# Cross-attention and expert layer: constants awaited singly, input loads reordered, two products moved ahead

## The reference

```python
kv   = ctx @ W_k.T + b_k                      # (b, 512, 128)
out  = layernorm(x) @ kv                      # (b, 512, 128)
sim  = out @ kv.T * 512 ** -0.5               # (b, 512, 512)
sim  = (sim - mean(sim)) * rsqrt(var(sim) + 1e-6) * ln_gamma + ln_beta
x    = x + softmax(sim)
n    = layernorm(x)
s, i = top_k(n @ Wg.T, 2);  w = softmax(s)    # two experts for each row
x    = x + sum_e w[e] * ((silu(n @ W1[e].T) * (n @ W2[e].T)) @ W3[e].T)
```

## Time and profile before

| | |
|---|---|
| Median of three runs | 385.76 us (385.14 to 386.96) |
| Profiled execution | 385.42 us, span 383.4 us |
| PE busy | 360.2 us, 94% of the span |
| DVE, ACT, POOL busy | 251.5, 234.5, 165.3 us |
| Chain that ended last | PE 77%, POOL 6%, issue 6%, DVE 4%, DMA 3%, ACT 2% |
| DMA | 57.61 MB, mean 150 GB/s |
| Mean granted clock of TensorE | 0.956 |

### The profile page before, as it was taken

One profiled execution on the slowest core, in us unless ns is written; L12 is line 12 of the kernel. 1 busy time (PEld: TensorE's weight loads), 2 busy tenths in 40 slices (PEclk: granted clock), 3 DMA queues, 4 the chain that ended last, 5 costly groups with the idle time before them and its releaser, 6 DMA issues.

```text
span 383.4 us, 8249 instructions
## 1 busy us (share of the span) xinstructions
PE 360.2 (94%) x2348; PEld 240.3 (63%) x2348; DVE 251.5 (66%) x647; ACT 234.5 (61%) x412; POOL 165.3 (43%) x193
## 2 busy tenths in 40 slices
PE   6889999998997999999999999999999999999981
PEld 5556767677965566566666666666666666666640
DVE  1267858887567965766676767575757576766660
ACT  1246857666356988857565666666666666575750
POOL 2116664868815034254434343435252534343331
PEclk9999999997558999999999999999999999999996
DMA  6999999898923034435353535354544444453424
GB/s 231 398 418 304 363 414 332 320 303 274 370 102 84 28 57 69 99 55 96 73 100 67 107 62 109 62 106 62 105 68 99 70 97 80 89 82 86 82 29 55
DMA packets 22121, 57.61 MB, mean 150 GB/s; under 512 B 4864, under 2 KB 4992, under 8 KB 20544
## 3 DMA queue, kind: packets, MB, share of 16 engines
q0 software_dynamic: 8736, 20.53, 29.7%
q1 hardware_dynamic: 11184, 20.17, 14.8%
q10 hardware_dynamic: 2160, 16.38, 11.5%
HBM read 38.17 MB, written 18.91 MB: 149 GB/s over the span
## 4 chain that ended last, share of the span: by engine, by line
PE 77%; POOL 6%; issue 6%; DVE 4%; DMA 3%; ACT 2%; POOLq 1%; DVEq 0%; ACTq 0%
PE bank L1308 36%; PE bank L1329 16%; PE bank L1299 4%; PE bank L1148 4%; PE bank L1319 3%; PE bank L1351 3%; PE bank L1169 2%; PE bank L1191 2%; PE bank L1057 2%; PE bank L1203 1%; DMA ng_s<-n_table,gidx 1%; DMA out<-kvj_s,sidx 1%; POOL rstd L429 1%; PE bank L1140 1%; POOL wrow L457 1%
## 5 line engine op out<-in xcount | busy, mean ns | idle before, releaser
L1308 PE MATMUL bank<-Wp,kvg_s 128*128 x480 | 78.2, 313 | 1.7 <-DVE kvg_s L1001 1.5
L995 DVE SCALAR_TENSOR_TENSOR stage<-W,w3sc,stage 128x512 f16<-128x512 f16 x99 | 71.1, 746 | 5.7 <-ACT stage L674 5.7
L1308 PE MATMUL bank<-Wp,kv_s 128*128 x456 | 74.3, 313 | 0.3
L1329 PE MATMUL bank<-stage,n_s 128*128 128x512 f16 (+1 forms) x297 | 69.6, 379 | 1.5 <-issue 1.5
L674 ACT ACTIVATE stage<-W,w3sc 128x512 f16 x99 | 67.3, 716 | 0.7 <-DVE w3sc L985 0.7
L1308 PEld LDWEIGHTS bank<-Wp,kvg_s 128*128 128x128 f16 x480 | 46.7, 98 | 29.0 <-issue 4.4
L526 POOL DMA_INDIRECT out<-oT_s,sidx x20 | 31.7, 1587 | 72.4 <-ACT oT_s L705 61.3
L1308 PEld LDWEIGHTS bank<-Wp,kv_s 128*128 128x128 f16 x456 | 44.4, 98 | 26.1 <-issue 2.7
L526 POOL DMA_INDIRECT out<-kvj_s,sidx x19 | 30.0, 1581 | 65.8 <-ACT kvj_s L705 63.4
L1022 DVE TENSOR_TENSOR n_s<-bank,n_s 128x384 f16<-128x384 f32 x33 | 18.4, 558 | 55.0 <-ACT n_s L687 53.3
L510 POOL DMA_INDIRECT ng_s<-n_table,gidx x39 | 41.2, 1056 | 22.2 <-issue 11.3
(11 more groups left out here) (196 smaller groups left out, 556.7 us busy)
## 6 DMA issues: line engine op xcount, KB each, us to landing
Wp<-in_w ACTq DMA_DIRECT2D x7, 1408.0 KB, 8.9
W<-in_w ACTq DMA_DIRECT2D x8, 768.0 KB, 6.6
W<-in_x SPq DMA_DIRECT2D x12, 256.0 KB, 9.7
out<-W SPq DMA_DIRECT2D x12, 256.0 KB, 8.6
stage<-in_xT SPq DMA_DIRECT2D x2, 1024.0 KB, 7.8
Wp<-in_xT SPq DMA_DIRECT2D x2, 1024.0 KB, 9.3
n_table<-n_s SPq DMA_DIRECT2D x8, 256.0 KB, 6.0
n_table<-x_s SPq DMA_DIRECT2D x8, 256.0 KB, 8.4
```

The lines of the kernel that those rows point to most:

```text
L995: eng.scalar_tensor_tensor(w3p[r][:, W3N + c * D:W3N + (c + 1) * D], W3[:, bass.ds(e * W3N + c * D, D)], w3sc[:, bass.ds(e, 1)], w3p[r][:, ...
L1308: mm = eng.matmul(bank[2 * which + r][:, 0:H], n_, w_, start=(c == 0 and k == 0), stop=(c == DC - 1 and k == 2))
L1329: mm = eng.matmul(ybank(t)[:, :], h_, w_, start=(c == 0 and k == 0), stop=(c == HC - 1 and k == 2))
```

## The change

Five edits:
- POOL makes `ones16` first, and TensorE starts its warm-up after one constant; it waits for all of them behind the warm-up. The counts in POOL's and ACT's waits go up by one.
- SP's key group is loaded in the order bias, context, weights. `w12[0]` is loaded ahead of x row 2 and no longer behind `wg_s`; `xT[1]` goes behind x row 2.
- For batch 0, both `outs` come before `gram` on TensorE, and `o_evac` before `gram_copy` on ACT.
- `squares(0)` comes before `sims(0, 1)` in slot n = 0.
- `weight_gram(0)` comes before `turn_keys(1)` in slot n = 1.

```diff
-            for dst, src in ((wk_s[:, :], wkT), (ctx_s[:, 0:N], ctxT[:, 0:N]), (bk_s[:, :], bk)):
+            for dst, src in ((bk_s[:, :], bk), (ctx_s[:, 0:N], ctxT[:, 0:N]), (wk_s[:, :], wkT)):
                 eng.dma_start(dst, src).then_inc(s_key, 16)
...
             for g in range(XAHEAD - 1):
                 if g == 2:
                     load_ctx(1)
+                    eng.dma_start(wst[0], w12[0]).then_inc(s_w[0], 16)
+                if g == 3:
                     eng.dma_start(xT_s[1], xT[1]).then_inc(s_xT[1], 16)
                 eng.dma_start(x_s[g], xrows[g]).then_inc(s_xl[g], 16)
             eng.dma_start(wg_s[:, :, :], wgT).then_inc(s_cin, 16)
-            eng.dma_start(wst[0], w12[0]).then_inc(s_w[0], 16)
             load_ctx(2)
...
         def _(eng):
+            eng.memset(ones16[:, :], 1.0).then_inc(s_const, 1)
             eng.memset(ident[:, :], 0.0).then_inc(s_const, 1)
...
-            eng.wait_ge(s_const, 6)
+            eng.wait_ge(s_const, 7)
...
-            eng.memset(ones16[:, :], 1.0).then_inc(s_const, 1)
...
-            eng.wait_ge(s_const, 4)
+            eng.wait_ge(s_const, 5)
             eng.activation(spare_a[:, 0:1], half[:, :], ACT.Exp)
...
             kvj_evac(0)
+            o_evac(0)
             gram_copy(0)
-            o_evac(0)
             batches(slot)
...
                 ba, ia = lead(b, i, 2)
+                if n == 0:
+                    squares(0)
                 if real(ba) and i != 2:
                     sims(ba, ia)
-                if i == 3 and real(b + 1):
+                if i == 3 and real(b + 1) and n > 0:
                     squares(b + 1)
                 if i == 3 and real(b + 2):
                     keys(b + 2)
+                if n == 1:
+                    weight_gram(0, 0, W12N // P)
                 if i == 0 and real(b + 1):
                     turn_keys(b + 1)
...
                 for k, slots in enumerate(GRAM_SLOTS):
-                    if n in slots:
+                    if n in slots and k > 0:
...
+            eng.wait_ge(s_const, 1)
+            warm(ones16[:, :], WARM_START)
             eng.wait_ge(s_const, NCONST)
-            warm(ones16[:, :], WARM_START)
             eng.wait_ge(s_key, 16 * 3)
             keys(0)
             warm(ones16[:, :], 2 * WARM_SLOT)
             turn_keys(0)
             warm(ones16[:, :], WARM_SLOT)
-            gram(0)
             outs(0, 0)
             outs(0, 1)
+            gram(0)
             gram_outs(0)
             sims(0, 0)
             eng.wait_ge(s_cin, 16)
```

## The result

Four executions of the changed kernel took 391.9 to 393.43 us, median 392.78, beside 385.66 us of the kernel before (four executions, 385.14 to 386.96). The ratio is 1.0178 (95% interval 1.0146 to 1.021): slower by some 7 us. The prediction was 389.7 us, with a range of 384.2 to 393.0. The profiled execution took 392.89 us with a span of 391.0, against 385.42 and 383.4: 7.5 us more.

The account below looks back on a forecast made before the run. TensorE's chain was taken as the bound. Gate at 23.5, work 8.5 and clock 2.4 put outs of batch 1 at 34.4 against 30.13, 4.3 us later: 385.42 becomes 389.7 us, own range 388 to 391.5, wide range 384.2 to 393.0.

Parts of the forecast that it names:

- The gate: TensorE's wait for wg_s after sims(0,0): reached at 17.05, open at 23.5 us, bounds 20.4 and 23.7.
- The difference made by ACT's load: ACT's w12[1], 1408 KB, going ahead of wg_s would delay its landing by 3.3 us.
- lower end: Earliest landing of wg_s, 20.4 us, if w12[1] starts only after it; taken from w12[0]'s landing before.
- The Trainium skill's rule on packets: An engine drains some 9 to 17 descriptors per queue turn; w12[1] goes through whole, gate at 23.7.
- The clock: TensorE idle 6.4 us at the gate drops to half clock; 4.8 us to recover, cost 2.4, bounds 0 and 8.5.
- The sum: Start of outs of batch 1: 23.5 + 8.5 + 2.4 = 34.4 against 30.13, 4.3 us later.
- Nothing gives it back: After outs of batch 1, the 4.3 us delay should reach the end of the kernel.
- The clock stays down: Rival: half clock persists behind the gate; ten microseconds at half cost 5.0, 392.3 us; whole 8.5, 395.8; chance 0.12.
- The early start gains nothing with the gate closed: Warm-up after one constant starts TensorE 2.6 us earlier, but gains nothing if it then waits for wg_s.
- Squares and weight products first: Behind the gate, weight products cover the 1.64 us wait for kv_s; work to outs of batch 1 is 8.5 us.
- `outs` before `gram`: In batch 0, ACT copies oT_s under gram, saving another 0.3 us; sims(0,0) ends at 17.05.
- The rival of the small load passing: wg_s gets past the large loads, gate at 17.05; w12[1] then holds outs of batch 1: 381.9 us, chance 0.09.

Follow-up runs that it names:

- Numbers 1 and 2: Changed kernel with wg_s loaded ahead of the x rows: 383.76 us; changed kernel with the wait for wg_s moved to the first router product: 383.61 us.
- number 6: Changed kernel with ACT's issue of w12[1] moved from the head to the end of its slot 0: 394.03 us in one execution.
- number 5: Kernel before with only w12[0] loaded ahead of x row 2 and xT[1] behind it: 388.17 us, ratio 1.0048.
- number 3: Changed kernel with 132 warm-up products between the first sims and the wait for wg_s: 389.55 us, ratio 1.0116.
- number 7: Changed kernel with wg_s loaded ahead of the x rows and the 48 warm-up products again behind all constants: 385.07 us, ratio 0.9985.
- number 11: Kernel before with only ones16 made first and the 48 warm-up products behind one constant: 383.67 us, ratio 0.9953.
- number 10: Changed kernel with wg_s ahead of the x rows, and sims(0,1) ahead of squares(0), turn_keys(1) ahead of weight_gram(0) again: 382.85 us.
- number 1: Changed kernel with the 16 KB load of wg_s issued ahead of the x rows: 383.76 us, ratio 0.9948.
- number 9: Changed kernel with wg_s ahead of the x rows, w12[1] issued before ACT's copy of outs, and more warm-up around the first gather: 381.22 us.

## Why the prediction was right or wrong

The measured median lies 3.1 us above the forecast, outside the narrower range of 388 to 391.5 us and 0.2 us inside the edge of the wide one. The mechanism was right. Two terms of the sum were too small, and one loss was not in it.

- *The gate*: right in place, cause and sign. Numbers 1 and 2 show it from two sides. Sized 23.5, measured 24.85, beyond my upper end of 23.7. The difference made by ACT's load was right (3.3 forecast, 3.4 in number 6), and so was its start (first packets at 18.3 forecast, 18.5 measured). Too low was the lower end: 20.4 forecast, 20.70 measured in number 5 (where 0.10 MB of `w12[1]` had gone) and 21.45 in number 6. I took it from `w12[0]`'s landing with the same bytes ahead. That assumes that a load lands when the bytes ahead of it and its own have moved, and these come to 5.98 MB. At the landing the queue had moved more: 6.50 MB for `w12[0]` before, 6.54 for `wg_s` in number 5, 6.79 in number 6 and 6.83 in the changed kernel. So parts of the loads behind had passed already. The 0.25 MB by which numbers 5 and 6 differ are 0.6 us at the 0.4 MB a microsecond that the queue moved there. Why more passed in one than in the other stays open.
- *The Trainium skill's rule on packets* (DMA: Bandwidth & Descriptors, Queues, rings and completion order): by the rule and by my value all of `w12[1]` went ahead, and that came true: q10 moved 1.39 of the load's 1.44 MB in 18.5:22.5, before `wg_s` landed. The counts don't tell whether the two queues took turns packet by packet or in longer turns, neither these (128 against 193) nor those of the earlier trace rows, from which the prediction reads "close to one by one".
- *The clock*: right that it falls, and number 3 shows that it costs. The mis-sized term is how long it stays down behind the gate: 4.8 us taken from the warm-up at the start, 6.8 measured; cost 3.4 and not 2.4, and 3.3 by number 3. The 4.8 us was one sample of a time that varies: the same 48 products took 5.11 us before and 4.41 in the changed kernel, and behind the gate of number 6 the clock was back after 5.3 us. So the kind of work behind the gate is not shown to be what made it longer. The Trainium skill (TensorE: Matmul & The Clock Gate, What's actually happening) calls the lower clock the default state, released by activity, and the prediction says that the rows of 90 us agree. They don't: TensorE was busy for 26.46 of 27 us at 0.51.
- *The sum*: 34.4 forecast for `outs` of batch 1, 36.71 measured; 1.35 from the gate, 1.0 from the clock. The work itself, 8.5, was right: number 3 has it at full clock, 8.50.
- *Nothing gives it back*: right, 6.58 us at 36.71 became 7.5 at the end. That something is added behind, the short fall of the clock at 127 us (0.9 us), was no step of mine.
- *The clock stays down* (0.12): this rival's 392.3 is nearest to the measured time, but not by its own sum: it had 5.0 us for the clock and 23.5 for the gate.
- *The early start gains nothing with the gate closed*: too mild. With it ACT issues `w12[1]` before `wg_s` has passed; in number 5, without it, the gate opened at 20.7 and not at 24.85. With the gate open it is worth 1.3 us (number 7); alone, with the old loads and 0.7 us of wait at the gate, 2 us (number 11).
- *Squares and weight products first*: counted at 1.6 us of TensorE's time; that wait is gone. With the gate open the order was worth 0.36 us at `outs` (number 10), since `w12[1]` was due next. In the changed kernel it lay behind the gate, which is why the sum could keep it.
- *`outs` before `gram`, and the new order of the key group*: neither was tried alone. Both act ahead of the gate, where TensorE came at 17.3 (17.05 forecast).
- *The rival of the small load passing*: its premise was false, but its consequence was checked by number 1: forecast 381.9, measured 383.8.

## What to carry to other kernels

Before moving anything earlier, list the waits that cost nothing today and their slack in us; a full stop for a small load behind large ones (2.9 us of slack here) turns into the longest wait of the kernel's first 120 us when the engine comes sooner and the load later. Look also at which other engine's loads an earlier start lets in ahead of it. Put a wait where the data is read, or the 16 KB ahead of the 1408. And price an idle stretch of TensorE at more than its length: here 7.6 us of idle cost another 3.3 us at half clock.

## What the runs showed of the hardware

- With both queues full, the queue whose data packets are of 11 KB moved 1.39 MB in 4 us (128 packets), and the one with packets of mostly 2 KB moved 0.27 MB (193). A load in the second queue is delayed by loads of an engine that has nothing to do with it: by 3.4 us in number 6.
- A load on ACT's queue had its first packets 3.5 us after its issue while SP's queue was full (3.6 before and in number 5), and 1.0 us after it in number 6, issued at 27.0 with the DMA engines idle.
- Behind three waits the clock was down: 7.6 us in the changed kernel, 4.1 us in number 6, and the 2.5 us for an expert weight in number 6, which ended at 32.9 (0.80 in 33:34, 0.50 in 34:36). Behind the wait of 1.3 us in number 5's profile it was not.
- The way back to full clock took 6.8 us behind the gate and 5.3 us in number 6. In number 9's profile, as in the kernel before, some 27 us passed at half clock with TensorE busy nearly all the time (28.46 of 29 us over 86:115, mean granted clock 0.53).
